# A decoder block in float32: cross-attention and up products in 16 double steps instead of 32 single ones

## What is computed

```python
x = x + attn(layernorm(x))                       # 16 heads of 128, biases, output projection
x = x + gamma * xattn(layernorm(x), ctx, ctx)    # 8 heads over the rows, see below
x = x + ffn(layernorm(x))                        # ternary weights, hidden 1365

# xattn(q, k, v): rows are the head dimension, columns are the positions
qh, kh, vh = q.reshape(B, 8, 64, 512), k.reshape(B, 8, 64, 512), v.reshape(B, 8, 64, 512)
sm  = softmax(einsum('bhdq,bhdl->bhql', qh, kh) / 8)
ret = einsum('bhql,bhdl->bhdq', sm, vh)

# ffn(x): w1q, w3q, w2q are sign patterns times a mean
g = silu(x @ w1q.T) * (x @ w3q.T)
out = g @ w2q.T
```

## Time and profile before

| | us |
|---|---|
| median of 3 runs | 1120.11 (1119.44 to 1120.29) |
| profiled execution, own time | 1120.62 |
| its span, first to last instruction | 1118.8 |
| TensorE busy | 1107.1 |
| VectorE busy | 731.1 |
| ScalarE busy | 541.9 |
| GpSimd busy | 478.5 |
| granted TensorE clock, mean | 0.998 |

### The profile page before, as it was taken

One profiled execution on the slowest core, in us unless ns is written; L12 is line 12 of the kernel. 1 busy time (PEld: TensorE's weight loads), 2 busy tenths in 40 slices (PEclk: granted clock), 3 DMA queues, 4 the chain that ended last, 5 costly groups with the idle time before them and its releaser, 6 DMA issues.

```text
span 1118.8 us, 15806 instructions
## 1 busy us (share of the span) xinstructions
PE 1107.1 (99%) x5804; PEld 939.0 (84%) x5804; DVE 731.1 (65%) x1357; ACT 541.9 (48%) x1129; POOL 478.5 (43%) x420
## 2 busy tenths in 40 slices
PE   7999999999999999999999999999999999999998
PEld 6888888878888888888888888888888888888886
DVE  7555547787857579865524244579967976887532
ACT  3455673323243265677425142167727762775130
POOL 0322326440432265674352140148637762875130
PEclk9999999999999999999999999999999999999999
DMA  7465554544443733412630202461113211310000
GB/s 245 162 183 187 168 179 142 176 125 152 133 134 94 240 104 90 130 46 85 251 113 1 76 9 96 156 204 49 45 60 114 76 48 57 104 58 2 38 1 38
DMA packets 54663, 122.19 MB, mean 109 GB/s; under 512 B 10057, under 2 KB 10057, under 8 KB 52538
## 3 DMA queue, kind: packets, MB, share of 16 engines
q1 hardware_dynamic: 54586, 121.18, 33.2%
HBM read 103.32 MB, written 17.84 MB: 108 GB/s over the span
## 4 chain that ended last, share of the span: by engine, by line
PE 95%; DVE 3%; issue 1%; ACT 1%; DMA 0%; SPq 0%; DVEq 0%
PE bank L161 19%; PE bank L162 19%; PE bank L163 19%; PE bank L567 7%; PE bank L568 7%; PE bank L525 5%; PE bank L583 4%; PE bank L582 4%; PE bank L549 3%; PE bank L550 3%; PE bank L535 3%; PE bank L536 2%; PE bank L592 0%; DVE x3l L844 0%; PE bank L1244 0%
## 5 line engine op out<-in xcount | busy, mean ns | idle before, releaser
L567 PE MATMUL bank<-x3h,w 128*128 128x512 f32 (+2 forms) x368 | 143.0, 392 | 0.4 <-DVE x3l L844 0.3
L568 PE MATMUL bank<-x3l,w 128*128 128x512 f32 (+2 forms) x368 | 140.3, 384 | 0.0
L1424 ACT ACTIVATE yh<-bank 128x512 fp32r<-128x512 f32 x64 | 38.1, 600 | 209.9 <-PE bank L163 209.8
L2030 POOL TENSOR_TENSOR wal<-raw_a,wah 128x512 fp32r<-128x512 f32 x44 | 60.5, 1402 | 137.5 <-ACT wah L1446 137.5
L924 POOL TENSOR_SCALAR pe_x<-pe_x,xri,gam 128x512 f32<-128x512 f32 x96 | 75.5, 787 | 78.7 <-DVE xri L763 76.1
L759 DVE TENSOR_REDUCE xmx<-bank 128x1 f32<-128x512 f32 x128 | 87.6, 686 | 32.8 <-PE bank L536 31.6
L2035 POOL TENSOR_TENSOR wbl<-raw_b,wbh 128x512 fp32r<-128x512 f32 x64 | 87.6, 1393 | 36.5 <-ACT wbh L1467 36.1
L161 PE MATMUL bank<-wah,gh 128*128 128x512 f32 x256 | 102.7, 401 | 0.0
L161 PE MATMUL bank<-yh,rh 128*128 128x512 f32 x256 | 100.2, 391 | 0.8 <-DVE xacc L1892 0.8
L161 PE MATMUL bank<-wah,ph 128*128 128x512 f32 x256 | 100.2, 392 | 0.0
L162 PE MATMUL bank<-wal,gh 128*128 128x512 f32 x256 | 100.2, 391 | 0.0
(11 more groups left out here) (168 smaller groups left out, 3000.5 us busy)
## 6 DMA issues: line engine op xcount, KB each, us to landing
raw_a<-in_wk SPq DMA_DIRECT2D x8, 1024.0 KB, 5.5
raw_b<-in_wq SPq DMA_DIRECT2D x8, 1024.0 KB, 6.6
raw_a<-in_wo SPq DMA_DIRECT2D x8, 1024.0 KB, 5.2
raw_b<-in_wvt SPq DMA_DIRECT2D x8, 1024.0 KB, 5.1
ternary_scratch<-wraw SPq DMA_DIRECT2D x24, 341.2 KB, 3.0
x1d<-x_scratch SPq DMA_DIRECT2D x48, 128.0 KB, 2.9
kd<-in_ctx SPq DMA_DIRECT2D x48, 128.0 KB, 2.9
w<-ternary_scratch SPq DMA_DIRECT2D x2, 2730.0 KB, 10.9
```

Of the source, the lines that this page charges most:

```text
L567: pe.matmul(u_bank[w][0:m, cols], lhs, x3h[:, c, cols], start=c == 0, stop=False)
L568: mm = pe.matmul(u_bank[w][0:m, cols], lhs, x3l[:, c, cols], start=False, stop=c == CK - 1)
L2030: pool.tensor_tensor(wal[:, c, :], raw_a[:, c, :], wah[:, c, :].bitcast(F32), ALU.subtract).then_inc(s["wal_pool"], 1)
```

## The change

The 32 single steps of a turn become 16 double steps (`STEPS`), each with two query tiles of a head. On TensorE a step now has the scores of both tiles, the transposes of the same two tiles of the head before, the up pieces of the step, and in each second step (tiles 2 and 3) the whole output of the head before, 8 matmuls of 512 columns. `r_ready` counts heads and no longer halves for items 1 to 3, so `r_done` gives the count to wait for. The pieces are spread over 16 steps; tanh runs in the step of its piece, between the exponentials of the two tiles; gates run at the head of the next step. VectorE takes both maxima, then both low parts, then the first reciprocal, the up pieces, the output of head h-2 (in even steps) and `dve_q`. The second tile's reciprocal opens the next step, on GpSimd its product does. The query copy opens ScalarE's odd step after the gate; GpSimd's preparation follows the first share of the odd step. No arithmetic is left out or added.

```diff
+        STEPS = 2 * XH
         def values_step(h):
-            return 4 * h + 2 if h else 1
+            return 2 * h + 1 if h else 0
         def prep_step(h):
-            return 4 * h if 0 < h < XH - 1 else None
+            return 2 * h if 0 < h < XH - 1 else None
+        def r_done(b, h):
+            return 2 * h + 2 if b == 0 else 2 * XH + (b - 1) * XH + h + 1
         def pieces(n):
-            return range(U_PIECES * n // S_TILES, U_PIECES * (n + 1) // S_TILES)
+            return range(U_PIECES * n // STEPS, U_PIECES * (n + 1) // STEPS)
+        def pe_ret_whole(pe, m, b, h):
+            pe.wait_ge(s["t_free"], t_p(b, h, 3) + 1)
+            if h % 2 == 0:
+                pe.wait_ge(s["vtl"], b * V_TILES + h // 2 + 1)
+            pe_wait(pe, "r_free", b * XH + h, 1)
+            for c in range(CK):
+                lhs = m.vts[:, h % 4, c, :]
+                pe.matmul(m.r[:], lhs, m.pxh[:, c, :], start=c == 0, stop=False)
+                mm = pe.matmul(m.r[:], lhs, m.pxl[:, c, :], start=False, stop=c == CK - 1)
+            mm.then_inc(s["r_ready"], 1)
         def pe_turn(pe, b, f, nxt):
+            for n in range(STEPS):
+                h, q = n // 2, n % 2 * 2
+                if b is not None:
+                    for k in (q, q + 1):
+                        pe_sx(pe, main, b, h, k)
+                    if h:
+                        for k in (q, q + 1):
+                            pe_pt(pe, main, b, h - 1, k)
+                if f is not None:
+                    for piece in pieces(n):
+                        pe_up(pe, f, piece)
+                if b is not None and h and q:
+                    pe_ret_whole(pe, main, b, h - 1)
...
         def act_turn(act, b, f, nxt):
+            for n in range(STEPS):
+                h, q = n // 2, n % 2 * 2
                 if f is not None:
-                    for piece in pieces(n - TANH_LAG):
+                    for piece in pieces(n - 1):
+                        act_gate(act, f, piece)
+                if b is not None:
+                    if prep_step(h) == n - 1:
+                        act_queries(act, main, b, h + 1)
+                    if h:
+                        for k in (q, q + 1):
+                            act_px(act, main, b, h - 1, k)
+                    act_exp(act, main, b, h, q)
+                if f is not None:
+                    for piece in pieces(n):
                         act_tanh(act, f, piece)
                 if b is not None:
-                    if h:
-                        act_px(act, main, b, h - 1, q)
-                    act_exp(act, main, b, h, q)
+                    act_exp(act, main, b, h, q + 1)
                     if prep_step(h) == n:
                         act_keys(act, main, b, h + 1)
...
         def dve_turn(dve, b, f, nxt, between=None):
+            for n in range(STEPS):
+                h, q = n // 2, n % 2 * 2
                 if b is not None:
+                    if n:
+                        dve_rinv(dve, main, b, (n - 1) // 2, (n - 1) % 2 * 2 + 1)
+                    for k in (q, q + 1):
+                        dve_max(dve, main, b, h, k)
+                    if h:
+                        for k in (q, q + 1):
+                            dve_px(dve, main, b, h - 1, k)
+                    dve_rinv(dve, main, b, h, q)
                 if f is not None:
-                    for piece in pieces(n - TANH_LAG):
+                    for piece in pieces(n):
                         dve_up(dve, f, piece)
                 if b is not None:
+                    if q == 0 and h >= 2:
+                        dve_ret(dve, main, b, h - 2)
                     if prep_step(h) == n:
                         dve_q(dve, main, b, h + 1)
-                    if q == 3 and h >= 4 and h % 2 == 0:
+                    if q and h >= 4 and h % 2 == 0:
                         dve_moments(dve, main, b, (h - 4) // 2)
                     if between:
-                        between(n)
+                        between(2 * n)
+                        between(2 * n + 1)
...
         def pool_turn(pool, b, f, nxt):
+            for n in range(STEPS):
+                h, q = n // 2, n % 2 * 2
+                if b is not None and n:
+                    pool_prob(pool, main, b, (n - 1) // 2, (n - 1) % 2 * 2 + 1)
+                if f is not None:
...
+                    for piece in pieces(n - 1):
+                        pool_up(pool, f, piece)
                 if b is not None:
+                    pool_prob(pool, main, b, h, q)
                     if prep_step(h) == n - 1:
                         pool_prep(pool, main, b, h + 1)
```

More of the change, by code:

```diff
@@ L595, in pe_turn @@
         def pe_turn(pe, b, f, nxt):
[L596 to L599, removed]
-                        if h:
[L601 to L608, removed]
+            for n in range(STEPS):
[11 more added lines that the diff above has]
+                    pe_ret_whole(pe, main, b, h - 1)
             if b is not None:
                 pe_pt(pe, main, b, XH - 1, 0)
-                pe_ret(pe, main, b, XH - 2, 1)
                 pe_pt(pe, main, b, XH - 1, 1)
@@ L616, in pe_turn @@
                 pe_pt(pe, main, b, XH - 1, 2)
+                pe_pt(pe, main, b, XH - 1, 3)
             if f is not None:
@@ L619, in pe_turn @@
             if b is not None:
-                pe_pt(pe, main, b, XH - 1, 3)
-                pe_ret(pe, main, b, XH - 1, 0)
+                pe_ret_whole(pe, main, b, XH - 1)
             if f is not None:
[L623 to L627, removed]
+                pe_down(pe, f, 1)
                 pe_down(pe, f, 2)
@@ L669, in act_vt @@
             else:
-                act.wait_ge(s["r_ready"], 2 * (b * XH + h - 3) + 2)
+                act.wait_ge(s["r_ready"], r_done(b, h - 3) if h >= 4 else r_done(b - 1, XH + h - 3))
             act.activation(high, values, ACT.Copy).then_inc(s["vth"], 1)
@@ L705, in act_turn @@
         def act_turn(act, b, f, nxt):
-            for n in range(S_TILES):
-                h, q = n // 4, n % 4
+            for n in range(STEPS):
+                h, q = n // 2, n % 2 * 2
                 if f is not None:
-                    for piece in pieces(n - TANH_LAG):
+                    for piece in pieces(n - 1):
[9 more added lines that the diff above has]
+                    for piece in pieces(n):
                         act_tanh(act, f, piece)
                 if b is not None:
-                    if h:
-                        act_px(act, main, b, h - 1, q)
-                    act_exp(act, main, b, h, q)
+                    act_exp(act, main, b, h, q + 1)
                     if prep_step(h) == n:
                         act_keys(act, main, b, h + 1)
[L717 to L723, removed]
-            if f is not None:
-                for n in range(S_TILES, S_TILES + GATE_LAG):
-                    for piece in pieces(n - TANH_LAG):
-                        act_tanh(act, f, piece)
-                    for piece in pieces(n - GATE_LAG):
-                        act_gate(act, f, piece)
+                    if h % 2 == 0 and values_step(h) == n:
+                        act_vt(act, main, b, h)
+            if f is not None:
+                for piece in pieces(STEPS - 1):
+                    act_gate(act, f, piece)
             if b is not None:
@@ L943, in pool_turn @@
         def pool_turn(pool, b, f, nxt):
-            for n in range(S_TILES):
-                h, q = n // 4, n % 4
+            for n in range(STEPS):
[3 more added lines that the diff above has]
+                if f is not None:
+                    if f and n < TJ // 2:
+                        pool_keep(pool, f, 2 * n)
+                        pool_keep(pool, f, 2 * n + 1)
+                    for piece in pieces(n - 1):
+                        pool_up(pool, f, piece)
                 if b is not None:
-                    if n:
-                        pool_prob(pool, main, b, (n - 1) // 4, (n - 1) % 4)
+                    pool_prob(pool, main, b, h, q)
                     if prep_step(h) == n - 1:
@@ L951, in pool_turn @@
                     if n - 1 in map(values_step, range(0, XH, 2)):
[L952 to L957, removed]
+                        pool_vt(pool, main, b, (n - 1) // 4 * 2)
             if b is not None:
@@ L960, in pool_turn @@
             if f is not None:
-                for n in range(S_TILES, S_TILES + GATE_LAG):
-                    for piece in pieces(n - GATE_LAG):
-                        pool_up(pool, f, piece)
+                for piece in pieces(STEPS - 1):
+                    pool_up(pool, f, piece)
             if nxt is not None:
```

25 lines of the change are left out of this document (5 added, 20 removed).

## The result

The changed kernel takes 1176.95 us (median of 4 runs, 1176.75 to 1178.03), the kernel before 1120.2: a ratio of 1.0506, 95% interval 1.0494 to 1.0519. It is slower by 57 us; 54.5 were forecast, inside a range of 1155 to 1190. The profiled execution has a span of 1175.9 us at clock 0.999.

A forecast was written before the change was run, and what follows sets the result against it. TensorE's own work bounds the kernel, but the next head's preparation becomes late: 1120.6 + 52.2 (three mixed turns) + 2.3 (small VectorE operations) = 1175.1, less 0.5 to the median: 1174.6 us, range 1155 to 1190.

The forecast's parts named there:

- TensorE's work: Matmuls and transposes on TensorE: whole outputs save 0.08 us per head, 1.9 us in all; pairing transposes saves nothing.
- the three that it named: TensorE's waits: some 31 us on the next head's preparation, 13 on exp, about 10 for outputs on the low shares.
- The preparation: Next head's serial chain over VectorE, ScalarE and GpSimd: ends late, making each mixed turn 17.4 us longer, three of them 52.2.
- Six head lengths: Heads 1 to 6, first score to first score: 13.25, 12.85, 13.5, 12.85, 15.35, 13.5, sum 81.3 us.
- X: Time after a head's first score when VectorE finishes normalising the next queries; the head lasts X + 6.35 us.
- the small chained operations: Two short VectorE operations ending each step of the first mixed turn, on the chain in six even steps: + 2.3 us.
- the tail: Turn's end (remaining shares, down products, x3): TensorE's order kept but for the whole output, costed at 0.
- the exp stalls: Second score waits for exp behind tanh, 1.14 us in four steps a turn; costs nothing further, preparation ends later.
- the output waits: Head outputs wait for the last low share, until X + 2.6; costs nothing further, since the preparation ends later.
- Nothing late: Rival: other engines have time to spare, TensorE's work alone decides, 1118.2 us; chance 0.07.
- only the exp stall: Rival: preparation is hidden, exp stalls alone cost 13.7 us, less 1.9: 1132 us; chance 0.07.
- The clock: Rival: holes drop TensorE from 2.4 to 1.2 GHz in one head of three, 47 us on top, 1222; chance 0.06.

The follow-up runs named there:

- e1: Changed kernel with GpSimd's preparation of the next head moved ahead of the odd step's first share: 1152.54 us.
- e3: Changed kernel with ScalarE's tanh moved behind the exponentials of both tiles of its step: 1180.82 us.
- e5: Changed kernel with GpSimd's preparation ahead of the first share and ScalarE's tanh behind both exponentials: 1153.41 us.
- e7: Changed kernel with preparation ahead of the share, queries normalised before the up pieces, output adds one step earlier, tanh behind both exponentials: 1135.49 us.
- e4: Kernel before, single steps kept, with only the whole head output of 8 matmuls of 512 columns: 1148.0 us.
- e8: Changed kernel with tanh behind both exponentials, plus 8 unused matmuls in step 11 of each mixed turn, ahead of the output's wait: 1178.24 us.

## Why the prediction was right

**The bound.** It said that TensorE's work decides, and that an order change can win nothing but can make an early thing late. The late things were the three that it named.

**TensorE's work.** The eight paired transposes take 894.27 - 893.48 = 0.79 us in the trace after, and the first matmul behind them 0.32 to the next: pairing is worth nothing, as said from the earlier trace rows.

```profile
893.48 1.03 PE L529 MATMUL bank<-ident,pe_x 128*128 128x128 f32 x8
894.27 0.48 PE L582 MATMUL bank<-x3h,w 128*128 128x512 f32 x1
894.59 0.39 PE L583 MATMUL bank<-x3l,w 128*128 128x512 f32 x1
```

The whole output's matmuls are 0.23 apart (median of the 56 in the second turn), as taken, so its gain on TensorE is near 0.08 a head; it was hidden in the waits and no run shows it by itself. The Trainium skill's formula (TensorE: Matmul & The Clock Gate, Back-to-back issue gap) gives 0.216 for such a matmul, which this trace does not bear out.

**The preparation.** Six head lengths were forecast to 0.03 us in four cases and to 0.27 in heads 3 and 5, sum 81.3 against 81.8. The exact hits are in part luck. The first two score matmuls after a wait are 0.33 apart, so the tanh began at 3.97 in place of 3.84 in head 3 and in head 6 alike. Yet head 6 came out right, since its VectorE steps were shorter than forecast:

```profile
939.36 0.69 DVE L799 SCALAR_TENSOR_TENSOR uu<-th,bank 128x512 f32<-128x512 f32 x1 [1.03 <-ACT th L701]
...
939.96 0.67 DVE L782 TENSOR_TENSOR x<-x,bank 64x512 f32<-64x512 f32 x1
...
940.67 0.69 DVE L784 TENSOR_TENSOR x<-x,bank 64x512 f32<-64x512 f32 x1
941.28 0.54 DVE L758 TENSOR_SCALAR x1d<-x1d,stx 128x512 f32<-128x512 f32 x1
```

From start to start these are 0.60, 0.71 and 0.61; in head 3, above, all three are 0.72. Heads 3 and 5 add the outputs of heads 1 and 3, whose rows are 64 to 127 of `x2`, the even heads those of rows 0 to 63, and the difference repeats in all three turns. It makes X 7.40 in head 3 where head 6 has 7.15, and X was late by as much in head 5 (9.25, 9.0 forecast). The forecast read its adds off one even head. That the chain is the cause, e1 shows by shortening it.

**The turns.** From first score to first score the second turn grew from 107.3 to 125.3 us, 18.0 (17.4 forecast); the first from 108.6 to 128.0, 19.4 (19.7 forecast, with the small chained operations); the third and fourth together by 18.6, of which the third has 18.1 and the last 0.5. Up to head 7's first transpose the second turn took 99.9 (99.1 forecast), and from there on 25.4, against 25.6 before (26.5 less the 0.95 of head 6's output): the tail cost nothing, as put down, although half a down group had moved behind the last transposes, which the prediction overlooked. 1 us lies ahead of the first turn. That the first turn was hit within 0.3 is luck: the small operations did lengthen its heads 1 to 6 by the 2.3 forecast (84.1 against 81.8 in the second turn), but before the change the same heads had already taken 1.1 more than those of the second turn, 1.0 of it at a wait in head 2 that the prediction left out:

```profile
PE bank L549 <- DVE x L774: 0.7, 1, 0.7
```

**Stalls that cost nothing.** The claim that the exp stalls lie in parallel with the preparation holds by e3: without them, head lengths stay. That holds only as long as the preparation is late; e3, e5 and e7, each against the kernel without the tanh move, show the exp stalls priced at 0, at 1.0 a turn in heads 3 and 6, and at 2 a turn. For the output waits no run shows the claim by itself.

**The rivals.** "Nothing late" and "only the exp stall" (1118, 1132) fall with the 34 us of waits on L928. The clock did not fall in the changed kernel: 1.00 in the stretches of its turns, with starts up to 2.35 us apart. With holes of 1.6 to 3.2 us it did fall in e3, e4, e5 and e8, each fall costing up to 2 us and all of them far from the 47 that I had put on this rival. The row that stood against it, that eight transposes at 838 us had run at clock 1.00, did hold: in the changed kernel eight transposes stand close behind each of the 18 waits on `ql`, at full clock. By the Trainium skill (TensorE: Matmul & The Clock Gate, Part 4: PE-mode transpose) they don't count as busy; no run here shows that they brought the clock down.

## What to carry to other kernels

Before two steps are merged, lay the longest chain that crosses engines on a clock with the new queue positions, and compare it with the bound engine's work per round; here 13.5 us against 10.7, and the six lengths came out to 0.3 us. Idle engines are no safety: a 2-line swap on GpSimd, 40% busy, was worth 24 us. And price each stall by what else is late in the same round: one and the same edit cost 4 us, gave nothing, and gave 6, depending on what came last.

## What the runs showed of the hardware

VectorE's steps around an add of 64 rows took 0.72 us from start to start where the adds wrote rows 64 to 127 (head 3 of the changed kernel), and 0.60, 0.71 and 0.61 where they wrote rows 0 to 63 (head 6), with the same kinds of instruction ahead of and behind them; a plan that goes by one of the two is off by 0.24 us in three steps. Why, no run shows.

TensorE's clock fell from 2.4 to 1.2 GHz (0.43 from matmul to matmul in place of 0.23, over some 3 to 7 us) behind single holes of 2.33 (e8), 2.85 (e3, twice) and 3.24 us (e3, e5), but also, in e4, behind 0.69 and 1.60 us and behind 0.71 and 1.77 us, with two matmuls between the holes of each pair. It did not fall behind a hole of 2.35 us in the changed kernel, behind 2.85 us twice in e5, or behind 0.7 and 1.77 us in the second turn of e4. So in these runs the length of a hole alone does not say whether the clock falls; what else decides, they do not show. With eight matmuls of no use in the hole of step 11 it stayed up in three turns out of three, where it had fallen in three out of three (e8 and e3, one profiled execution each). So a wait of 2 to 3 us can cost 2 us more than its own length, and removing a small stall ahead of a large one can bring that on.
